# A convolution whose normalised inputs stay in token order, read by TensorE 32 bytes apart

## The reference

```
A_bar = exp(DT * -exp(log_A));  K[d, l] = sum_n C[d, n] * B_bar[d, n] * A_bar[d, n]^l
y = irfft(rfft(K) * rfft(x_t))[:seq_len] + D * x_t          # channel by channel
```

## Time and profile before

| | us |
|---|---|
| median of 3 runs | 5113.91 (5109.72 to 5118.38) |
| the profiled execution | 5112.74 |
| its span | 5111.0 |
| TensorE busy (PE) | 4492.4, 88% |
| VectorE busy (DVE) | 2908.1, 57% |
| ScalarE busy (ACT) | 2464.0, 48% |
| GpSimd busy (POOL) | 797.2, 16% |

### The profile page before, as it was taken

The page is one execution under the profiler, slowest core; times in us unless marked ns, Lnnn a source line. Parts: engine busy times, 40 slices in busy tenths (PEclk is TensorE's granted clock), DMA queues, the critical chain, the costliest instruction groups (busy, mean ns, idle before and its releaser), DMA issues. The chain is left out here.

```text
span 5111.0 us, 84445 instructions
## 1 busy us (share of the span) xinstructions
PE 4492.4 (88%) x30530; PEld 3760.8 (74%) x30530; DVE 2908.1 (57%) x5365; ACT 2464.0 (48%) x5934; POOL 797.2 (16%) x648
## 2 busy tenths in 40 slices
PE   6666657999999999999999999743999999999999
PEld 6555546888888888888888888542777777777776
DVE  5666644555555555555555555578556556556555
ACT  4554533555555555555555555422434434434434
POOL 0000001122122122122122122210011111111111
PEclk9987768999999999999999999755999999999999
DMA  6877761000000000000000000100120110120110
GB/s 216 233 205 203 202 169 33 29 26 30 28 28 30 30 26 30 30 26 30 30 26 30 30 26 18 50 0 17 34 48 18 37 47 18 36 48 18 36 40 11
DMA packets 288343, 284.03 MB, mean 56 GB/s; under 512 B 15216, under 2 KB 213104, under 8 KB 287984
## 3 DMA queue, kind: packets, MB, share of 16 engines
q1 hardware_dynamic: 275696, 245.55, 16.7%
q0 software_dynamic: 12288, 33.56, 3.0%
HBM read 186.27 MB, written 76.02 MB: 51 GB/s over the span
## 5 line engine op out<-in xcount | busy, mean ns | idle before, releaser
L1164 POOL TENSOR_TENSOR l_prob<-l_prob,l_inv 128x768 f32<-128x768 f32 x256 | 370.5, 1469 | 1922.2 <-DVE l_inv L1107 1922.2
L954 ACT ACTIVATE l_prob<-l_ps_s,l_neg_max 128x192 f32<-128x192 f32 (+1 forms) x1024 | 411.8, 428 | 362.6 <-DVE l_neg_max L1091 362.2
L1942 ACT ACTIVATE h_prob<-h_ps_s,h_neg_max 128x1024 f32<-128x1024 f32 x256 | 285.9, 1117 | 341.4 <-DVE h_neg_max L2024 310.3
L2021 DVE TENSOR_REDUCE h_neg_max<-h_ps_s 128x1 f32<-128x1024 f32 x256 | 313.2, 1223 | 201.7 <-PE h_ps_s L1808 199.7
L690 PE MATMUL l_ps_b<-w_qkv_hi,l_xt_hi 128*128 128x512 f32 x1024 | 417.9, 408 | 5.6 <-DVE l_xt_lo L1011 2.9
L691 PE MATMUL l_ps_b<-w_qkv_lo,l_xt_hi 128*128 128x512 f32 x1024 | 406.4, 397 | 0.0
L692 PE MATMUL l_ps_b<-w_qkv_hi,l_xt_lo 128*128 128x512 f32 x1024 | 406.4, 397 | 0.0
L851 PE MATMUL l_ps_s<-l_k_t,l_q_t 128*128 128x192 f32 (+2 forms) x2432 | 377.7, 311 | 18.1 <-issue 13.2
L851 PEld LDWEIGHTS l_ps_s<-l_k_t,l_q_t 128*128 128x128 f32 x2432 | 354.4, 192 | 26.9 <-issue 26.9
L1117 DVE TENSOR_TENSOR l_q_t<-l_ps_a,w_bias_q 64x512 f32<-64x512 f32 x256 | 176.3, 689 | 263.2 <-PE l_ps_a L841 260.5
L1820 PE MATMUL h_ps_t<-ident,h_prob 128*128 128x128 f32 x2048 | 277.4, 278 | 7.6 <-ACT h_prob L1942 7.6
(11 more groups left out here) (360 smaller groups left out, 11305.5 us busy)
## 6 DMA issues: line engine op xcount, KB each, us to landing
xin<-in_L_attn_x_dram SPq DMA_DIRECT2D x32, 1024.0 KB, 5.2
xg<-in_L_attn_x_dram SPq DMA_DIRECT2D x64, 512.0 KB, 7.8
toep_back<-taps_padded SPq DMA_DIRECT2D x32, 1024.0 KB, 7.0
x<-xg SPq DMA_DIRECT2D x64, 512.0 KB, 7.4
l_xin<-x SPq DMA_DIRECT2D x128, 256.0 KB, 3.9
out_dram<-l_res SPq DMA_DIRECT2D x128, 256.0 KB, 3.2
ea_all<-in_L_attn_log_A_dram SPq DMA_DIRECT2D x32, 512.0 KB, 7.1
h_q_hi<-h_q_hi SPq DMA_DIRECT2D x64, 128.0 KB, 5.1
```

The costliest lines, as they stand in the source:

```text
L954: last = nc.scalar.activation(prob[jt % 2][:, pair, AT[win] + lo:AT[win] + hi], ps_s[:, win, pair, lo:hi], ACT.Exp, bias=neg_max[:, jt % 2 ...
L1164: nc.gpsimd.tensor_tensor(mine, mine, spread(inv[:, jt % 2, win, :], [1, PAIRS], [0, MAIN + SIDE]), ALU.mult).then_inc(p_normed, 1)
L1942: nc.scalar.activation(prob[i % 2][:, :].rearrange("p (a k) -> p a k", a=2), ps_s[i % 2][:, :, :], ACT.Exp, bias=neg_max[:, qt % 2, h:h + ...
L2021: nc.vector.tensor_reduce(at, ps_s[i % 2][:, :, :].rearrange("p a k -> p (a k)"), AX_X, ALU.max, negate=True).then_inc(max_step, 1)
```

## The change

`centred` goes. `xn` has a new shape: half, sequence, chunk, channel of the half (8). L412 writes its difference straight into `xn` in that order, and L415 multiplies `xn` in place, all three of its operands in the order of the source; `rstd` is now spread in the way `mean` was, each value repeated for 8 channels. TensorE's products L540 and L557 get their moving operand from `channel(par, ch)`: 128 columns with a step of 8 elements, 32 bytes. The wait of the centring for the scaling before it (`normed`) goes, as `centred` was its reason. The number of instructions of each kind is the same.

```diff
-        xn = [sb(f"xn{i}", [P, SUB, COLS]) for i in range(2)]
-        centred = sb("centred", [P, BATCH, NCH, SUB // 2])
+        xn = [sb(f"xn{i}", [P, 2, BATCH, NCH, SUB // 2]) for i in range(2)]
...
-        def by_column(a):
-
-            return spread(a[:, :], [0, SUB // 2], [1, COLS])
...
-                    dst = xn[par][:, h * HALF:(h + 1) * HALF, :]
-                    if not (isinstance(it, int) and it * 2 + h == 0):
-                        v.wait_ge(normed, it * 2 + h)
-                    nc.vector.tensor_tensor(centred[:, :, :, :], src, spread(mean[:, :], [NCH, BATCH], [1, NCH], [0, HALF]),
+                    dst = xn[par][:, h]
+                    nc.vector.tensor_tensor(dst, src, spread(mean[:, :], [NCH, BATCH], [1, NCH], [0, HALF]),
                                             ALU.subtract).then_inc(norm_step, 1)
                     v.wait_ge(norm_step, it * 2 + h + 1)
-                    nc.vector.tensor_tensor(dst, centred[:, :, :, :].rearrange("p b c d -> p d (b c)"), by_column(rstd),
+                    nc.vector.tensor_tensor(dst, dst, spread(rstd[:, :], [NCH, BATCH], [1, NCH], [0, HALF]),
                                             ALU.mult).then_inc(normed, 1)
...
+                def channel(par, ch):
+                    return xn[par][:, ch // (SUB // 2), :, :, ch % (SUB // 2)].rearrange("p b c -> p (b c)")
...
-                                                    tail[:, ch * STATE:(ch + 1) * STATE], xn[par][:, ch, :],
+                                                    tail[:, ch * STATE:(ch + 1) * STATE], channel(par, ch),
...
-                                nc.tensor.matmul(ps_y[f][:, i, :], toep[par][:, ch, :], xn[par][:, ch, :],
+                                nc.tensor.matmul(ps_y[f][:, i, :], toep[par][:, ch, :], channel(par, ch),
```

## The result

The changed kernel takes 5136.76 us (median of 5 runs, 5132.26 to 5142.54), the kernel before 5117.73 us (median of its 5 runs with it, 5109.72 to 5119.55). The ratio is 1.004, 95% interval 1.0028 to 1.0051. Forecast were 5081 us and, with 0.68, faster. The profiled execution took 5133.43 us (span 5131.7), 20.7 us more than that of before.

A forecast was written before the change was run, and what follows sets the result against it. The convolution was taken as bound by a chain through VectorE and TensorE, 13.7 us a period, apart from transfer-set stretches. Gains of 29 us plus 3 for the clock, 32 off 5112.74, gave 5081 us; range 5060 to 5132.

The forecast's parts named there:

- VectorE's part: Scaling in the convolution: 64 instructions from 2.04 to 1.23 us, 0.8 us less each, 1.6 us an interval.
- the sum: Convolution: 25.6 us in 16 free intervals, less 1, plus 4.8 in the last stretch, gives 29 us.
- the clock: TensorE in the convolution idles less, so gets its low clock less often: 0.15 us an interval, 3 us in all.
- rival D: Convolution: transfers take up the gain, log_A rows come too late in 6 intervals, 10 us lost: 5091; chance 0.12.
- The cost of TensorE's reads: Products L540 and L557 reading columns 32 bytes apart: 0 to 10 ns more a record, 119 ns kept for the range.
- the half rate: TensorE's fp32 record asks for an element half as often as the engine can take one: 0.91 against 0.45 ns a column.
- TensorE's own row: Profile row of TensorE's 512-column products, one every 0.23 us, 0.45 ns a column; basis for 0 to 10 ns.
- Rival A: Convolution: TensorE pays for spaced reads at VectorE's 235 ns a record, 14.7 us a period, +19 us: 5132; chance 0.23.
- The break-even of 60 ns: Extra price per TensorE record in the convolution at which 40x - 0.8 equals the 1.6 us gain; slower from there.

The follow-up runs named there:

- e1: Changed kernel, but each TensorE product reads 128 adjacent columns of xn (wrong elements): 5090.48 us against 5116.6 for the kernel before, ratio 0.995.
- e4: Kernel before, with xn holding two channels side by side, scaling reading two elements at a time, TensorE reading 8 bytes apart: 5081.67 us against 5116.6, ratio 0.9937.
- e9: Changed kernel, L553's products replaced by fp32r ones of 512 moving columns, at steps of 1, 2, 3, 4 elements by bank: 5131.69 us, one run.
- e5: Changed kernel, but L553's four banks read at steps of 1, 2, 3 and 4 elements (wrong elements): 5091.03 us, one run.
- e6: Changed kernel, but L553's banks read at steps of 6 and 7 elements, in pairs every 32 bytes and in fours every 64 bytes: 5112.15 us, one run.
- e3: Kernel before, but the centring writes spaced into xn (512 bytes apart), scaling in place and TensorE's reads dense: 5110.31 us, ratio 0.9991.

## Why the prediction was wrong

- *VectorE's part* was right: 1.23 us for 2.04, 0.8 on the chain for each half. Where it stands alone (e1), the convolution ends 30.6 us earlier in the trace, and the medians differ by 26 (17 to 34), where the sum had 29, and 32 with the clock. The sum missed two things that take a little back: an earlier VectorE meets GpSimd's copy more often (24 slowed instructions in e1, 11 before, some 0.6 us each), and part of the first stretch is then set by the tails (rival D), with intervals of 13.3 to 13.7 us in e1 where others take 12; TensorE waits for tails in 19 steps there and 20 in e4, 16 in the earlier trace rows.
- *The cost of TensorE's reads* is the step that failed. I took "0 to 10 ns" a record, and it is 112. The argument was that the fp32 record asks for an element half as often as the engine can take one, so that a slow fetch would hide in the second half of each column's time. Its two rows are right; what doesn't follow is that the fetch has room. e9 shows a spaced column of the fast kind at 0.89 ns, about twice its dense 0.46, and e5 shows one of the fp32 kind at 1.7 ns, twice its own 0.87. Each kind about doubles, and the half rate hides nothing. What in the engine makes it so stays open.
- I called "TensorE's own row", but it shows dense reads only. The one row with the operation in question, a read with one hit a line, was VectorE's: 1.83 ns an element. TensorE's is 1.74. Here the nearest row was the one of the same access, not the one of the same engine. That the two numbers lie so close may be luck: for fp32r products VectorE's row would have been twice too high.
- *The rule of the Trainium skill* (Advanced Engine Details and Errata, section SBUF Cachelines: lines of 16 bytes, two hits needed) was cited as speaking against the change, and it did. e5 and e6 agree with it for fp32: 114 ns where two columns share a line, 209 to 233 where none do. For fp32r it doesn't hold: step 2 has two hits a line and costs 0.89 ns a column in e9, as step 4.
- *Rival A* had the mechanism, the place and nearly the time: 14.7 us a period (measured 14.7), +19 us (measured 19 to 21), and the new wait ahead of the second centring. Its parts were less good than its sum: +1.0 in 19 intervals was +11.7 us in 16 and +2.9 in the last stretch, less 2.0 in those of the transfers, and I had left out the tail behind the last scan, where TensorE alone sets the pace and loses 6.3 us. That the sum of +19 came out is luck in so far as the tail made up for the intervals. The break-even of 60 ns in the same rival is a wrong sum: 40x - 0.8 charges the full x to the first sixteen records of L557, which the period beside it rightly charges 235 - 210 = 25 ns each. At x = 119 the line would give a loss of 2.4 us an interval, the period gives 1.0, and 1.0 was measured. A had only 0.23 because of the argument on the half rate that failed, and the range ended on A's price with nothing above.
- *The clock.* That the idle gaps shrink and the upper level is granted more was right, 0.93 for 0.79, and is worth nothing here. It counts where the reads are adjacent: over the 32 steps the first sixteen records of L553 take 144 ns each on average in e1 and 174 before, some 0.5 us a step, where the sum had 0.15. A spaced fp32 record takes nearly the same time at either level: the 32 spaced records of L536 below take 3.49 us in a stretch with a granted clock of 1.00 and 3.55 in one with 0.50.

```profile
196.68 3.49 PEld L536 LDWEIGHTS ps_state<-xn,tail 128*64 128x64 f32 x32 [19.79 <-ACT tail L465]
...
385.24 3.55 PEld L536 LDWEIGHTS ps_state<-xn,tail 128*64 128x64 f32 x32 [8.11 <-issue]
```

```profile
196.70:200.50 3.80, 3.80 (x32) 2.98 (x32) 3.73 (x4) 3.29 (x12) 0.00 (x0) 1.00 0.53 163
385.20:389.00 3.80, 3.76 (x32) 3.38 (x32) 0.00 (x0) 3.39 (x12) 0.00 (x0) 0.50 1.13 334
```

This is also why the loss is no larger: before, the first sixteen records of an interval ran in part at the lower level, at 210 ns each in the earlier trace rows and 174 on average over the 32 steps, and so lose 48 ns each by the spacing. The second sixteen, at 111 ns in every step, lose 112.

## What to carry to other kernels

A layout that saves one engine a spaced access and gives it to another saves nothing until both prices are known, and a row of the same engine without the access pattern doesn't give its price; a row with that pattern on another engine was the better guess here, and the pattern on the engine itself, in a small experiment, is the price. For fp32 operands, keep two neighbours together in each 16 bytes: side by side in pairs, both engines read at full speed here, and that beat both kernels by 0.6% and 1%. When a change frees an engine, add up the stretches in which the other one works alone as well; they pay the new price in full.

## What the runs showed of the hardware

- A column that TensorE reads from a 16-byte stretch of its own costs 1.6 to 1.8 ns in an fp32 record (0.87 dense; e5, e6), with the pairs side by side in two halves of the array not slower (32 records of L536 in 3.49 us). Two columns to a stretch cost 0.88 to 0.89, as dense (e5, e6).
- In an fp32r record of 512 columns a column costs 0.89 ns at steps of 2, 3 and 4 elements alike (0.46 dense; e9).
- The spaced price of an fp32 record is a time, not a number of the array's cycles: 32 records of L536 take 3.55 us at a granted clock of 0.50 and 3.49 at 1.00.
- VectorE pays for spaced writes as for spaced reads: 2015 ns (e3) and 2043 ns for 1024 elements, 1225 dense.
- Beside a GpSimd copy the scaling of 1.23 us took 1.89 us (16 of 64 in e1), a centring of 1.2 us 1.6 to 2.0, though not every one that overlaps a copy (8 of 27).
